# Graph attention on one core: two adjacency loads in a row on SyncE, with the store and the first turn behind them

## The reference

```python
# x (4096, 128) f32, adj (4096, 4096) int32, Wq/Wk/Wv (128, 128), biases (128,)
q, k, v = x @ Wq.T + bq, x @ Wk.T + bk, x @ Wv.T + bv
scores = where(adj > 0, q @ k.T / sqrt(128), -9e15)
att = softmax(scores, axis=-1) @ v
y = x + elu(att)
out = (y - mean(y)) / sqrt(var(y) + 1e-5)        # per row
```

## Time and profile before

| | before |
|---|---|
| median of 3 runs | 427.45 us |
| the profiled execution's own time | 428.24 us |
| its span | 426.4 us |
| TensorE busy (matmul) | 415.8 us, 97% |
| VectorE / ScalarE / GpSimd busy | 360.3 / 353.6 / 353.0 us |
| share of the DMA engines used by SP's queue | 91.8% |
| adjacency loads | 63 of 1 MB, 2 of 0.5 MB |
| turns by DMA | 63 |

### The profile page before, as it was taken

One profiled execution on the slowest core, in us unless ns is written; L12 is line 12 of the kernel. 1 busy time (PEld: TensorE's weight loads), 2 busy tenths in 40 slices (PEclk: granted clock), 3 DMA queues, 4 the chain that ended last, 5 costly groups with the idle time before them and its releaser, 6 DMA issues.

```text
span 426.4 us, 11467 instructions
## 1 busy us (share of the span) xinstructions
PE 415.8 (97%) x3470; PEld 310.5 (73%) x3470; DVE 360.3 (84%) x677; ACT 353.6 (83%) x742; POOL 353.0 (83%) x644
## 2 busy tenths in 40 slices
PE   7998999999999999999999999999999999999994
PEld 6764777777777777777777777777777777777793
DVE  3788888988888898888888988888889888888774
ACT  5888688898888888988888889888888988888883
POOL 0596578988898889888988898889888988898875
PEclk9999999999999999999999999999999999999999
DMA  8944999999999999999999999999999999998541
GB/s 245 402 167 92 260 265 281 260 272 281 275 245 266 266 273 267 243 272 273 263 244 274 272 261 242 272 266 267 252 271 270 269 241 271 269 265 224 105 81 43
DMA packets 149793, 104.77 MB, mean 246 GB/s; under 512 B 132754, under 2 KB 141460, under 8 KB 141716
## 3 DMA queue, kind: packets, MB, share of 16 engines
q1 hardware_dynamic: 149344, 104.41, 91.8%
q10 hardware_dynamic: 436, 0.20, 0.2%
HBM read 69.47 MB, written 2.10 MB: 168 GB/s over the span
## 4 chain that ended last, share of the span: by engine, by line
POOL 59%; issue 17%; PE 8%; DMA 6%; ACT 4%; POOLq 2%; SPq 2%; DVE 1%; ACTq 0%; DVEq 0%
POOL p_rows L410 27%; POOL res L424 6%; POOL var_eps L446 4%; DMA p_turned<-p_rows 4%; POOL rstd L448 4%; POOL y L429 3%; POOL att_sum L417 3%; POOL neg_mean L435 3%; POOL att L419 3%; POOL centred L437 2%; POOL expm L426 2%; DMA x_rows<-in_x_dram 2%; PE ps_out L975 2%; POOL y_out L452 2%; ACT scores L550 1%
## 5 line engine op out<-in xcount | busy, mean ns | idle before, releaser
L410 POOL TENSOR_TENSOR p_rows<-scores,p_rows 128x256 f16<-128x256 f32 x252 | 176.9, 734 | 9.9 <-ACT p_rows L567 9.3
L697 DVE CUSTOM_DVE_ANT_0 scores<-ps_scores,adj 128x1024 f32<-128x1024 f32 x128 | 155.8, 1218 | 11.5 <-issue 8.8
L550 ACT ACTIVATE scores<-scores,neg_max 128x1024 f32<-128x1024 f32 x128 | 145.9, 1140 | 3.0 <-DVE neg_max L707 3.0
L713 DVE TENSOR_TENSOR p_lo<-ps_t,p_hi 128x512 f16<-128x512 f32 x124 | 82.4, 685 | 30.3 <-ACT p_hi L559 30.2
L683 DVE TENSOR_SCALAR adj<-adj 128x1024 f32<-128x1024 int32 x128 | 102.7, 805 | 1.1 <-DMA adj<-in_adj_dram 1.0
L935 PE MATMUL ps_scores<-k_hi,q_hi 128*128 128x512 f16 x256 | 97.0, 379 | 0.0
L936 PE MATMUL ps_scores<-k_lo,q_hi 128*128 128x512 f16 x256 | 97.0, 379 | 0.0
L937 PE MATMUL ps_scores<-k_hi,q_lo 128*128 128x512 f16 x256 | 97.0, 379 | 0.0
L975 PE MATMUL ps_out<-v_parts,p_turned 128*128 128x256 f16 x496 | 95.0, 273 | 0.3 <-DMA p_turned<-p_rows 0.2
L975 PE MATMUL ps_out<-v_parts,p_hi 128*128 128x256 f16 x496 | 95.1, 273 | 0.0
L977 PE MATMUL ps_out<-v_parts,p_lo 128*128 128x128 f16 x496 | 88.5, 219 | 0.0
(11 more groups left out here) (121 smaller groups left out, 477.4 us busy)
## 6 DMA issues: line engine op xcount, KB each, us to landing
adj<-in_adj_dram SPq DMA_DIRECT2D x63, 1024.0 KB, 5.3
out_dram<-y_out SPq DMA_DIRECT2D x32, 64.0 KB, 4.8
x_rows<-in_x_dram SPq DMA_DIRECT2D x4, 256.0 KB, 4.5
x_rows<-in_x_dram SPq DMA_DIRECT2D x2, 512.0 KB, 7.5
adj<-in_adj_dram SPq DMA_DIRECT2D x2, 512.0 KB, 7.5
p_turned<-p_rows SPq DMA_TRANSPOSE x63, 4.4
w_rows<-in_L_gnn_Wq_dram ACTq DMA_DIRECT2D x1, 64.0 KB, 2.7
w_rows<-in_L_gnn_Wk_dram ACTq DMA_DIRECT2D x1, 64.0 KB, 3.4
```

Source lines behind the costliest of these rows:

```text
L410: last = nc.gpsimd.tensor_tensor(p_rows[c][:, w:][:, cols], s_sb[s][:, c * PIECE:c * PIECE + w][:, cols], p_rows[c][:, 0:w][:, cols], ALU. ...
L550: nc.scalar.activation(s_sb[s][:, cols], s_sb[s][:, cols], ACT.Exp, bias=neg_max[:, s:s + 1], accum_out=p_sums[:, s, c:c + 1]).then_inc(ex ...
L697: nc.vector.tensor_tensor_reduce(out=s_sb[s][:, cols], in0=ps_scores[c % 2][:, :], in1=mask_sb[s][:, cols], scale=SCALE, scalar=-3.0e38, o ...
L713: nc.vector.tensor_tensor(p_lo[:, k, :], ps_t[bank_of(s, g)][:, :], p_hi[:, k, :], ALU.subtract).then_inc(plo_ready, 1)
```

## The change

Inside SP's `period`, the load of half 0 of block p+2 moves from the end to directly behind the load of half 1 of block p+1. Nothing else differs.

```diff
                 if head:
                     load_half(p + 1, 1 - n, 1, False)
+                if loads:
+                    load_half(p + 2, n, 0, False)
                 if stores:
                     store(p - 4, n)
                 if turns_0:
                     turn(p - 1, 1 - n, 0)
-                if loads:
-                    load_half(p + 2, n, 0, False)
```

## The result

The changed kernel takes 439.02 us (median of 4 runs, 438.67 to 441.3) against 427.41 us (median of 4, 427.33 to 427.82): the ratio is 1.027, 95% interval 1.0245 to 1.0295. It is slower, as forecast (435.3 us, range 427.0 to 450).

The account below looks back on a forecast made before the run. TensorE's 12.20 us a period was taken as the bound; +7.0 (loop) + 1.3 - 0.5 (start) = +7.8 us on the profiled 428.24 us gave 436.0, with the median 0.79 lower, 435.3 us; range 427.0 to 450 us.

Parts of the forecast that it names:

- What bounds the kernel: Middle of the kernel: TensorE is busy all 12.20 us of each 12.20 us period, so earlier loads cannot shorten it.
- The load of half 0: SP's queue, middle: issued 3.2 us earlier, at about 205.85 us; worth 0 us because TensorE is full.
- the store: SP's queue: moves about 3 us to behind the load; gates only reuse of `y_out` two blocks later, so 0 us.
- X: DMA queue: time from the load's issue to the first turn's landing, taken as 7.86 us, bounds 7.0 to 9.19 us.
- the three: Turns closely behind a load near the start: 7.86, 7.46 and 9.19 us from load's issue to turn's landing.
- The loop: First turn, group 0, scores, mask, load, next first turn: 4.6 + X, 12.46 us a period against TensorE's 12.20.
- 27 periods x 0.26: Periods from 4 up to 30: the loop adds 0.26 us to each, 7.0 us in all.
- The first periods: Start: TensorE waits 1.3 us once for block 1's group 0; 0.5 us given back as ScalarE's 2.8 us wait goes.
- Rival 1: Middle: the two loads overlap and the turn arrives in time, X = 7.0 us, no change, 427.4 us; chance 0.33.
- Rival 2: Start gives back all 1.09 us and X stays under 6.6 us from period 3: 426.35 us; chance 0.09.
- Rival 3: All turns land 9.19 us behind the load, period 13.79 us, 472 us; a mix gives 445 us; chance 0.07.
- Rival 4: Change does not reach the turn, if the mask were ready well before the rows; no chance given.

Follow-up runs that it names:

- the run with the wait alone: Kernel before, order kept, but SP also waits for piece 1 of block p to be masked ahead of the first turn, no load ahead: 427.67 us, ratio 0.9994.

## Why the prediction was right, point by point

- **What bounds the kernel.** Right: TensorE's 12.20 us is the floor, and no kernel here got below it in the middle.
- **The load of half 0, worth 0 us by itself; the store, 0 us.** The first is right: no kernel with earlier loads is faster. The second nearly: the store gates nothing, but its place between load and turn costs about 0.15 us a period, which the kernel with the store ahead shows.
- **The turn: X = 7.86 us behind the load.** Measured 7.7 us to the landing, 7.76 to group 0; the average over the middle is 7.71. The side was right, but choosing this value was in part luck. The least of the three, 7.46 us, would have given no loop, and their mean, 8.17 us, a loop of 12.77. The same stretch of the trace has more turns shortly behind a load than the three listed. The first turn issued at 46.55 us, 0.77 us behind its load, gives 8.07 us; the second turns issued at 39.76, 52.49, 65.23, 77.16 and 89.52 us give 10.1, 9.4, 9.1, 9.3 and 7.5. The gap of 1.25 us was thus not shorter than all that the trace had. The forecast also gives X as 7.6 to 8.7 us in one place and ends its range at 8.4 in another. The turn's issue took 4.33 us where I had said over 3.5.
- **The loop: 4.6 + X.** The loop is there, group 0 starts when the turn lands. The term was mis-sized: 4.82 us. I took the end of TensorE's scores as VectorE's start; VectorE started at 209.11 us, 0.18 us later, since its `p_lo` step had waited 0.47 us for ScalarE, and SP took 0.19 us in place of 0.1. So 12.58 us in place of 12.46; X, a little over-sized, made up for part of it. "Before, the first turn depended on GpSimd only" left out that GpSimd's rows hang on the landing of the turn before: that is the loop that the load of half 1 closely ahead of the turn brought out.
- **27 periods x 0.26 = 7.0 us.** Measured 26 x 0.36 = 9.4 us. This is the largest part, 2.4 us, of the 3.7 by which the forecast was low; 0.9 are the start, and the rest is the difference between spans and medians.
- **The first periods: +1.3 and -0.5 us.** The sum of 0.8 us came out as 1.7, by another way than told. Group 0 of block 0 was late by 1.78 us, where I had expected nothing, and the wait I had put at block 1 didn't add to it: block 1 is 1.42 us late in all. ScalarE's wait of 2.8 us became 0.7 us, as told, and gave back 0.4 us at most.
- **The sum.** +7.8 us predicted, +11.1 us on the spans, +11.6 us on the medians. The range, 427.0 to 450 us, took in no change as well, so the number alone says less than the 12.58 us from group 0 to group 0.
- **Rival 1 (the loads overlap).** In the changed kernel the loads don't stand in a row in time: they leave 4.46 us apart (206.06 and 210.52), the first has nearly landed, and the second takes its full 5.4 us. Where they did leave close together, 1.74 us apart at the change of order, the turn landed 9.6 us behind the second load, later and not earlier. The Trainium skill ("DMA: Bandwidth & Descriptors", section "Anatomy of one DMA") gives its fixed part and its rate for DMAs issued from GpSimd, and these are issued from SyncE; by the estimate made from them X would have been 6.7 us, and no turn here within 1.3 us behind a load of 1 MB landed in less than 7.3 us from that load's issue.
- **Rival 2 (faster)** fell at the first turn, which was late and not early. **Rival 3**: 9.6 us behind the load was seen once, in the kernel that changes its order at period 4, and not throughout. **Rival 4** was excluded by the earlier trace rows, and the run with the wait alone shows that the two events do coincide.

## What to carry to other kernels

Where one queue carries both large loads and small transfers that an engine waits for, count the time from the issue of the load to the landing of the small transfer, and keep the load's issue well ahead of it or behind it (here 3.2 us ahead was enough for 1 MB, 1.2 us was not). Before moving an issue past another, write down every wait in front of it and follow the loop round and hold its length against the period of the engine that bounds the kernel: that tells whether the move is free. Two loops can run through the same transfer, so freeing one may only show the other.

## What the runs showed of the hardware that was not expected

- The price of a late transfer isn't linear in the wait. In the window of the changed kernel with waits under 1 us for a turn TensorE's clock is 1.00, and it stayed there after the 1.90 us at block 0. In the kernel with the store ahead of the load the same wait was 2.18 us and the clock was 0.50 from 43.0 to 46.4 us. Behind waits of 3.13 us, with 2 MB ahead, it was at the lower level for 3.4 us each time round, and a loop that should take 15.3 us took 17.1.
- The delay of the turn goes with the bytes ahead of it. With its nearest load issued 1.15 to 1.2 us ahead, the first turn landed on average 5.39, 6.55 and 8.74 us after its issue with 0.5, 1 and 2 MB (averages over the middle of three kernels; the 2 MB are two loads 0.55 us apart). With 1 MB 3.2 us ahead it is 4.37. These are 1.0, 2.2 and 4.4 us more, so some 2.2 us for each MB. No run issues the turn from another queue, so whether it is its place in SyncE's queue or the sharing of the DMA engines that counts is not told apart.
- A turn that has both a load 3.3 us ahead and another turn 2.5 us behind it landed 1.7 to 2.0 us later in three of four profiles, and with only one of the two in none of two. The cause is open.
